# A state-space scan on one core: handing over halves of a step (one PSUM bank, two states) in place of whole steps

## The reference, cut to what matters

```
dA  = exp(A[None, :, None, :] * dt_bdl[:, :, :, None])                      # decays
dBu = dt_bdl[:, :, :, None] * Bm[:, None, :, :] * hs[:, :, :, None]
def step(s, inp):
    a, bu = inp
    s = a * s + bu
    return (s, s)
_, h = jax.lax.scan(step, init, (dA_l, dBu_l))                              # over the 256 positions
y = jnp.einsum('lbdn,bln->bdl', h, Cm)                                      # products with C, summed over the states
y = y + hs * D[None, :, None]
y = y * _silu(gate)
out = jnp.einsum('bdl,od->blo', y, W_out)
```

## Time and profile before

| what | us |
|---|---|
| median of 3 runs | 3314.96 (3314.78 to 3315.2) |
| the profiled execution: its time | 3312.39 |
| its span | 3310.6 |
| state-space stage, to about | 1835 of the span |

### The profile page before, as it was taken

How to read it: one execution, slowest core, us unless ns; L and a number is a source line. 1 busy time by engine, 2 the same in 40 slices (tenths; PEclk the granted TensorE clock), 3 DMA queues, 4 the chain that set the end, 5 groups by cost and what they waited for, 6 DMA issues and landing times. The chain is left out here.

```text
span 3310.6 us, 46132 instructions
## 1 busy us (share of the span) xinstructions
PE 3024.3 (91%) x16101; PEld 1824.4 (55%) x16134; DVE 2788.9 (84%) x2773; ACT 2408.3 (73%) x4531; POOL 2094.7 (63%) x1207
## 2 busy tenths in 40 slices
PE   7899999999999999999987699999999999879998
PEld 5677667766776677667755234444444443234444
DVE  6999999999999999999999677788787777278886
ACT  4877787778777877788786167767767767667776
POOL 5999999999999999999999234434434433200000
PEclk9999999999999999999998799999999999989999
DMA  4102211221022102210221554655655653131111
GB/s 169 48 27 77 77 52 36 77 77 55 33 77 77 58 30 77 77 59 30 77 93 64 165 163 154 183 175 155 182 173 162 176 177 117 48 117 45 45 45 36
DMA packets 164376, 311.86 MB, mean 94 GB/s; under 512 B 22736, under 2 KB 80208, under 8 KB 164000
## 3 DMA queue, kind: packets, MB, share of 16 engines
q1 hardware_dynamic: 158784, 299.53, 28.1%
q10 hardware_dynamic: 5360, 9.38, 0.9%
HBM read 217.16 MB, written 91.69 MB: 93 GB/s over the span
## 5 line engine op out<-in xcount | busy, mean ns | idle before, releaser
L821 POOL TENSOR_TENSOR bu<-du,bc 128x1024 f32<-128x1024 f32 x512 | 1197.4, 2363 | 46.6 <-DMA bc<-bc_scratch 28.6
L699 ACT ACTIVATE states<-dt,negA 128x256 f32<-128x256 f32 x2048 | 852.3, 463 | 360.4 <-DVE hc L918 335.2
L905 DVE TENSOR_TENSOR_SCAN states<-states,bu 128x1024 f32<-128x1024 f32 x352 | 805.9, 2289 | 73.9 <-ACT states L699 72.5
L1558 DVE TENSOR_REDUCE mmax<-s_ps 128x2 f32<-128x1024 f32 x512 | 624.7, 1224 | 204.3 <-PE s_ps L1277 185.5
L1402 ACT ACTIVATE pt<-s_ps 128x512 f32<-128x512 f32 x1024 | 573.4, 598 | 293.2 <-PE s_ps L1286 280.6
L918 DVE TENSOR_TENSOR hc<-states,bc 128x1024 f32<-128x1024 f32 x352 | 431.0, 1224 | 41.1 <-DVE states L905 6.4
L519 PE MATMUL y_ps<-id_sb,hc 128*128 128x128 f32 x2816 | 381.7, 280 | 79.3 <-DVE hc L918 79.3
L519 PEld LDWEIGHTS y_ps<-id_sb,hc 128*128 128x128 f32 x2816 | 325.3, 143 | 205.7 <-DVE hc L918 166.8
L830 POOL TENSOR_TENSOR hp<-hp,bc 128x1024 f32<-128x1024 f32 x160 | 377.7, 2360 | 45.1 <-DVE hp L905 45.0
L1286 PE MATMUL s_ps<-qst,kst 105*128 105x512 bf16 x1024 | 378.6, 383 | 14.8 <-ACT pt L1402 5.1
L905 DVE TENSOR_TENSOR_SCAN hp<-states,bu 128x1024 f32<-128x1024 f32 x160 | 364.8, 2280 | 6.0 <-ACT states L699 6.0
(11 more groups left out here) (172 smaller groups left out, 4236.8 us busy)
## 6 DMA issues: line engine op xcount, KB each, us to landing
bc<-bc_scratch SPq DMA_DIRECT2D x128, 512.0 KB, 4.3
stack_d<-parts SPq DMA_DIRECT2D x180, 256.0 KB, 3.0
qst<-stack_d SPq DMA_DIRECT2D x64, 384.0 KB
kst<-stack_d SPq DMA_DIRECT2D x64, 384.0 KB
x<-xres SPq DMA_DIRECT2D x31, 512.0 KB, 4.3
w_raw<-in_w_ffn SPq DMA_DIRECT2D x48, 256.0 KB, 2.7
w_raw<-in_w_ffn SPq DMA_DIRECT2D x16, 768.0 KB, 7.4
xT_sb<-in_xT SPq DMA_DIRECT2D x16, 512.0 KB, 5.3
```

The costliest lines, as they stand in the source:

```text
L699: a = act.activation(states[:, bank, first:first + SEQ], dt[:, t, :], ACT.Exp, scale=negA[:, t, c * NS + n:c * NS + n + 1])
L821: pool.tensor_tensor(bu[:, buf, :].rearrange("p (n l) -> p n l", n=NS), du[:, t % (2 * GRP):t % (2 * GRP) + 1, :].to_broadcast([P, NS, SEQ ...
L905: m = dve.tensor_tensor_scan(dst, src, bu[:, BU_OF[k][0], half * 2 * SEQ:(half + n) * 2 * SEQ], 0.0, ALU.mult, ALU.add)
L1558: dve.tensor_reduce(mmax[:, u // HG, c:c + 2], s1_ps[:, pair], AX.X, ALU.max).then_inc(s1_free, 1)
```

## The change

The decays, the scans and the products of DVE are handed over in halves of 512 elements (one bank, two states). `decays` waits for each bank's last reader by itself and increments `decay_ready` after each two activations. A scan is two instructions of 512 elements, each with its own wait for its decays and its own increment of `scan_done`. The product on DVE is two instructions of 512, each with a wait for its half of the scan and for its half of the old sum, and an increment of `hc_dve` each. PE waits for each half of the product by itself, in front of its 4 matmuls, and increments `sum_dve` after each 4. The products on POOL, its bu and their sums stay whole and wait for the second half.

```diff
+HALVES = 2
+HALF = CHUNK // HALVES
+def bank_of_half(k, half):
+    return (HALVES * k + half) % BANKS
+BACK = BANKS // HALVES
...
+        def half_of(b, k, half):
+            return HALVES * (b * STEPS + k) + half + 1
+        def half_product(b, k, half):
+            return HALVES * (products(b, k) - 1) + half + 1
...  (PE, sum_states)
                 else:
-                    pe.wait_ge(hc_dve, products(b, k))
-                    src, done = hc[:, DVE_STEPS.index(k) % 2, :], sum_dve
+                    src = hc[:, DVE_STEPS.index(k) % 2, :]
                 for n in range(NS):
+                    if k not in POOL_STEPS and n % (NS // HALVES) == 0:
+                        pe.wait_ge(hc_dve, half_product(b, k, n // (NS // HALVES)))
                     for i in range(SEQT):
                         m = pe.matmul(y_ps[:, i, :], ...)
-                m.then_inc(done, 1)
+                    if k not in POOL_STEPS and n % (NS // HALVES) == NS // HALVES - 1:
+                        m.then_inc(sum_dve, 1)
...  (ACT, decays)
+                b0, k0 = (b, k - BACK) if k >= BACK else (b - 1, k - BACK + STEPS)
+                for half in range(HALVES):
+                    if not (isinstance(b, int) and b == 0 and k < BACK):
+                        if k0 in POOL_STEPS:
+                            act.wait_ge(scan_done, half_of(b0, k0, half))
                         else:
-                            act.wait_ge(hc_dve, products(b, before))
-                    for i in range(NS // 2):
+                            act.wait_ge(hc_dve, half_product(b0, k0, half))
+                    for i in range(NS // HALVES):
                         a = act.activation(states[...], dt[:, t, :], ACT.Exp, ...)
-                a.then_inc(decay_ready, 1)
+                    a.then_inc(decay_ready, 1)
...  (POOL, inputs and times_C: wait for half_of(b, ..., HALVES - 1))
...  (DVE, scan)
                 dve.wait_ge(bu_done, b * STEPS + k + 1)
-                dve.wait_ge(decay_ready, b * STEPS + k + 1)
...
-                for bank, half, n in runs_of(k):
-                    m = dve.tensor_tensor_scan(dst, src, bu[...], 0.0, ALU.mult, ALU.add)
-                m.then_inc(scan_done, 1)
+                for half in range(HALVES):
+                    cols, src = slice(half * HALF, (half + 1) * HALF), states[:, bank_of_half(k, half), :]
+                    dst = hp[:, POOL_STEPS.index(k) % 2, cols] if k in POOL_STEPS else src
+                    dve.wait_ge(decay_ready, half_of(b, k, half))
+                    dve.tensor_tensor_scan(dst, src, bu[:, BU_OF[k][0], cols], 0.0, ALU.mult, ALU.add).then_inc(scan_done, 1)
...  (DVE, times_C)
-                    dve.wait_ge(sum_dve, products(b, k) - 2)
-                dve.wait_ge(scan_done, b * STEPS + k + 1)
+                for half in range(HALVES):
+                    cols = slice(half * HALF, (half + 1) * HALF)
+                    if not (isinstance(b, int) and b == 0 and i < 2):
+                        dve.wait_ge(sum_dve, half_product(b, k, half) - 2 * HALVES)
+                    dve.wait_ge(scan_done, half_of(b, k, half))
+                    dve.tensor_tensor(hc[:, i % 2, cols], states[:, bank_of_half(k, half), :], bc[:, c, 1, cols], ALU.mult)\
+                       .then_inc(hc_dve, 1)
```

More of the change, by code:

```diff
@@ L68 @@
 PROJ = 7 - BANKS
[L71 to L78, removed]
+HALVES = 2
[3 more added lines that the diff above has]
+BACK = BANKS // HALVES
+assert STEPS % BACK == 0
 POOL_STEPS = (0, 4, 6, 10, 14, 16, 20, 22, 25, 28)
@@ L316, in unit_before @@
                     return kind, seq(kind, b - 1 + off, i)
-        def runs_of(k):
-            lo, hi = PAIRS_OF[k]
-            return [(lo, 0, 2)] if hi == lo + 1 else [(lo, 0, 1), (hi, 1, 1)]
+        def half_of(b, k, half):
+            return HALVES * (b * STEPS + k) + half + 1
+        def half_product(b, k, half):
+            return HALVES * (products(b, k) - 1) + half + 1
         def products(b, k):
@@ L433, in _ @@
                         sp.wait_ge(hc_pool, pool_products(b, max(k for k in POOL_STEPS if k % CPT == c or k == 0)))
-                        sp.wait_ge(hc_dve, products(b, max(k for k in DVE_STEPS if k % CPT == c)))
+                        sp.wait_ge(hc_dve, half_product(b, max(k for k in DVE_STEPS if k % CPT == c), HALVES - 1))
                         spread(c, 1, c_in)
@@ L512, in sum_states @@
                     pe.wait_ge(hc_pool, pool_products(b, k))
-                    src, done = hp[:, POOL_STEPS.index(k) % 2, :], sum_pool
+                    src = hp[:, POOL_STEPS.index(k) % 2, :]
                 else:
-                    pe.wait_ge(hc_dve, products(b, k))
-                    src, done = hc[:, DVE_STEPS.index(k) % 2, :], sum_dve
+                    src = hc[:, DVE_STEPS.index(k) % 2, :]
                 for n in range(NS):
+                    if k not in POOL_STEPS and n % (NS // HALVES) == 0:
+                        pe.wait_ge(hc_dve, half_product(b, k, n // (NS // HALVES)))
                     for i in range(SEQT):
@@ L521, in sum_states @@
                                       skip_group_check=True)
-                m.then_inc(done, 1)
+                    if k not in POOL_STEPS and n % (NS // HALVES) == NS // HALVES - 1:
+                        m.then_inc(sum_dve, 1)
+                if k in POOL_STEPS:
+                    m.then_inc(sum_pool, 1)
             def rows_by_tile(bank):
@@ L617, in tail @@
                 pe.wait_ge(w_added, BATCH)
-                pe.wait_ge(hc_dve, products(BATCH - 1, STEPS - 1))
+                pe.wait_ge(hc_dve, half_product(BATCH - 1, STEPS - 1, HALVES - 1))
                 for bank, parts in enumerate((range(GU_COLS // PART), range(GU_COLS // PART, W_PARTS))):
@@ L688, in decays @@
                     act.wait_ge(du_ready, b * GROUPS + t // GRP + 1)
[L689 to L694, removed]
-                        else:
-                            act.wait_ge(hc_dve, products(b, before))
-                    for i in range(NS // 2):
-                        n, bank, first = half * NS // 2 + i, PAIRS_OF[k][half], i * SEQ
+                b0, k0 = (b, k - BACK) if k >= BACK else (b - 1, k - BACK + STEPS)
[3 more added lines that the diff above has]
+                            act.wait_ge(scan_done, half_of(b0, k0, half))
+                        else:
+                            act.wait_ge(hc_dve, half_product(b0, k0, half))
+                    for i in range(NS // HALVES):
+                        n, bank, first = half * NS // HALVES + i, bank_of_half(k, half), i * SEQ
                         a = act.activation(states[:, bank, first:first + SEQ], dt[:, t, :], ACT.Exp,
                                            scale=negA[:, t, c * NS + n:c * NS + n + 1])
-                a.then_inc(decay_ready, 1)
+                    a.then_inc(decay_ready, 1)
             def norm_first():
@@ L819, in inputs @@
                 if not (isinstance(b, int) and b == 0 and before < 0):
-                    pool.wait_ge(scan_done, b * STEPS + before + 1)
+                    pool.wait_ge(scan_done, half_of(b, before, HALVES - 1))
                 pool.tensor_tensor(bu[:, buf, :].rearrange("p (n l) -> p n l", n=NS),
@@ L827, in times_C @@
                     pool.wait_ge(c_in[k % CPT], (b + 1) * 16)
-                pool.wait_ge(scan_done, b * STEPS + k + 1)
+                pool.wait_ge(scan_done, half_of(b, k, HALVES - 1))
                 h = hp[:, POOL_STEPS.index(k) % 2, :]
@@ L898, in scan @@
                 dve.wait_ge(bu_done, b * STEPS + k + 1)
-                dve.wait_ge(decay_ready, b * STEPS + k + 1)
                 if k in POOL_STEPS and pool_products(b, k) > 2:
                     dve.wait_ge(sum_pool, pool_products(b, k) - 2)
-                for bank, half, n in runs_of(k):
-                    src = states[:, bank:bank + n, :].rearrange("p i l -> p (i l)")
-                    dst = hp[:, POOL_STEPS.index(k) % 2, half * 2 * SEQ:(half + n) * 2 * SEQ] if k in POOL_STEPS else src
-                    m = dve.tensor_tensor_scan(dst, src, bu[:, BU_OF[k][0], half * 2 * SEQ:(half + n) * 2 * SEQ], 0.0, ALU.mult, ALU.add)
-                m.then_inc(scan_done, 1)
+                for half in range(HALVES):
[3 more added lines that the diff above has]
+                    dve.tensor_tensor_scan(dst, src, bu[:, BU_OF[k][0], cols], 0.0, ALU.mult, ALU.add).then_inc(scan_done, 1)
             def times_C(b, k):
@@ L912, in times_C @@
                 i = DVE_STEPS.index(k)
-                if not (isinstance(b, int) and b == 0 and i < 2):
-                    dve.wait_ge(sum_dve, products(b, k) - 2)
-                dve.wait_ge(scan_done, b * STEPS + k + 1)
[L916 to L920, removed]
+                for half in range(HALVES):
[5 more added lines that the diff above has]
+                       .then_inc(hc_dve, 1)
             def finish_y(b, par, t):
@@ L924, in finish_y @@
                     dve.wait_ge(gate_ready, b + 1)
```

(2 more changed lines are left out.)

## The result

The changed kernel takes 3224.46 us (median of 4 runs, 3222.66 to 3225.14) against 3314.87 (4 runs, 3311.38 to 3315.2): a ratio of 0.9729, 95% interval 0.9717 to 0.974. Its profiled execution has a span of 3222.1 us, 88.5 less than before.

What follows compares the result with a forecast made beforehand. DVE with its stalls sets the 109.88 us beat, POOL close behind; 109.75 - 4.1 - 1.7 + 0.8 = 104.7, plus 0.2 coupling is 104.9; 70 us in 14 batches plus 2 at each end gives 3241 us, range 3228 to 3283.

Steps and rivals of the forecast that it cites:

- The four stalls a batch on ACT: DVE's waits for ACT's decays, 37.7 us from 500 to 1500 us: all taken as gone, 4.1 us a batch.
- PE's gaps in the first half of a batch: PE's idle time from 1052.35 to 1104.14, some 2.9 us; ACT's earlier evacuations were to take back about 1.4.
- the slower rival: DVE's pipeline: added instructions lose their overlap, +2.4 us a batch, 3349 us; chance 0.08.
- plus 0.8 new: 104.7: DVE's beat: 103.95 us plus a new wait for PE of about 0.8 near yT of step 16 or 12.
- I add 0.2 for it: Coupling of DVE and POOL through four bu buffers: 0.2 us a batch added, giving a beat of 104.9.
- POOL's floor: POOL's own operations in a batch sum to 104.2 us, under which no faster DVE gets.
- the old 1.27: DVE's once-a-batch stall for PE's sums in front of yT, 1.27 us, forecast to stay.
- I take 2 us each, an estimate (between 0 and the 5 of a steady batch): First and last batches of the state-space stage: 2 us gained in each.
- the 2.6 us that I laid between profiled execution and median: Whole kernel: median of runs taken 2.6 us above the profiled execution, so 3238.4 became 3241.
- The range's low end: Whole kernel: POOL's 104.2 us as the beat, with 3.5 us at either end, 87 us gained, 3228 us.
- Net gain 1.7 us a batch: DVE's halving: 4.4 us from the removed bubble less 2.7 for 54 added instructions; bounds 0.1 to 3.3.
- the stalls stay: DVE's waits on ACT remain, only DVE's bubble goes: about 1.7 us a batch, 3291 us; chance 0.09.

Runs made afterwards that it cites:

- e6: Kernel before the change, with bu computed for only two of four states in steps 29 and 30 on POOL: 3311.67 us, ratio 0.9999.
- e10: Kernel before the change, with bu of step 12 computed twice on POOL (same values): 3313.86 us, ratio 1.0002.
- e2: Changed kernel, but decays are reported once a step, so a half scan needs all four; they still start bank by bank: 3252.92 us.
- e3: Changed kernel, but decays of both banks start when the second bank's last reader is over; still reported by halves: 3249.9 us.
- e7: Changed kernel with every half scan cut into two scans of 256 elements, 64 more DVE instructions a batch: 3252.5 us, ratio 0.9816.
- e5: Changed kernel with bu computed for only two of four states in steps 29 and 30 on POOL: 3221.02 us, ratio 0.9721.
- e1: Changed kernel with only DVE's instructions halved; ACT's decays wait for both halves, report once; PE waits for whole product: 3303.49 us.

## Why the prediction was wrong, point by point

- **The direction and the mechanism were right.** POOL's work was no bound before (e6, e10). The four stalls a batch on ACT are gone: of 37.7 us the early start alone leaves 21.2 (e2), the report by halves alone 8.7 (e3), both together none. An added instruction costs 0.045 to 0.055 us where 0.05 was booked (e7). In the changed kernel half products are 0.6 apart and half scans 1.12, the values named. PE's gaps in the first half of a batch fell from 2.9 us to 1.6: 1.3 came back where 1.4 was named. One reading was off without changing anything: a table load ends right in front of the decays of all four stalls, not of three.
- **The Trainium skill's rule** (VectorE: DVE Perf Modes, "The DRAIN you can't avoid"), as the prediction quotes it, would have every start cost a whole duration. The quarter scans last 0.67 us and start 0.58 apart, so here too they overlap by 0.09, and the slower rival fell. The same section goes on to say that a next operation which isn't held starts earlier, and the prediction left that out; read whole, it doesn't speak against this change, and the trace agrees with it.
- **The step that failed: the beat as a sum, "plus 0.8 new: 104.7" with "I add 0.2 for it".** POOL's floor was rightly summed up at 104.2, and 0.7 were then put on top of it. DVE's chain measures 104.1 (e5), not 104.7, so it lies under the floor and costs nothing, and the coupling costs next to nothing: POOL never waits for DVE. The beat is 104.18 in a steady batch and 104.30 over the fourteen, the first of which takes 105.37. 8 of the missing 16 us are this. The waits for PE aren't where the 0.6 of the chain went: with 1.62 and 0.41 they are 0.76 above the old 1.27, near the 0.8 booked. The net gain of the halving is 1.9 and not 1.7; the products had waited 4.1 us in the stretch for their own scans, 0.45 a batch, which the sum counts only as far as 0.10 a step and which is gone; and with POOL out of the way the second wait for PE is 0.24, not 0.41 (e5). How these add up to the 0.6 is not shown to the last tenth.
- **The ends, which put the result outside the range.** "I take 2 us each, an estimate (between 0 and the 5 of a steady batch)": they gave 3.5 and 6.6, the second above its own bound. In the last batch DVE's waits for decays fall from 4.7 us to 1.0, and POOL's for DVE and dt from 9.2 to 2.6, which is the size of the gain there; the trace of before had both, and I put an estimate in place of adding them up. That is 6 of the missing 16 us. The rest is the 2.6 us that I laid between profiled execution and median, which the changed kernel doesn't show (0.5). The range's low end took the floor as the beat and 3.5 us for either end. So the beat gave 1.7 us less than this end allowed for, but the ends gave 3.1 more and the 2.6 another 2.1: together, 3.1 + 2.1 - 1.7, the 3.5 by which it was missed.
- **A step that was right in sum only: "Net gain 1.7 us a batch" for the bubble.** The instructions are cheaper by that (1.9), but alone it brings 0.6 (e1), since DVE's stalls grow by nearly as much. It counts in full only where the stalls are gone, and there POOL's floor covers a part of it. So the rival "the stalls stay", which I put at 3291, would have been 3303.

## What to carry to other kernels

When an engine waits for another one that itself waited for the first, making the first cheaper can go into a longer wait, as 1.6 of 1.9 us did here (e1). Hand over smaller pieces first, so that the loop has slack, and only then count cheaper instructions. The slack comes from both sides of a hand-over, the earlier start and the smaller need; here each without the other, with the halved instructions in it, gave two thirds of the gain. And find the floor of the next engine by adding up its own operations start to start: where that floor lay over the chain that was freed, as here, the beat was the floor itself, with nothing on top. Add up the first and the last batch by their own waits too.

## What the runs showed of the hardware that was not expected

Two engines sit within 0.1 us of each other for 14 batches (104.2 for POOL, 104.1 for the chain of DVE) without a loss from their coupling. Put side by side, the timelines of the batch from 972 to 1076 us show how: POOL's bu is over 0.8 to 5.4 us before its scan starts, so the lead moves by some 4.6 us within a batch (worked out with even spacing inside each row) and never reaches nothing. The four buffers of bu hold it, and between 500 and 1500 us neither engine has a wait for the other.
